# Masked attention's inputs loaded during the quantised stage's second loop, and its preparation and loop made one block

## The chip, the cores and the metric

The kernel runs on one core of a Trainium2 chip. The metric is the device time of one execution in microseconds (us), lower being better; the runs give a median.

## What is computed

Four layers are applied in turn to x (2 sequences of 2048 rows of 512), each with a layer norm ahead and a residual add behind:

```python
x = x + _L0_xattn_ref(_layernorm(x), ctx_1024, ctx_1024, mask_BxS2_bf0, ...)    # rope attention, causal
x = x + _L0_ffn_ref(_layernorm(x), clip_x, clip_down, w_gate, w_up, w_down)     # quantised gated FFN
x = x + _L1_xattn_ref(_layernorm(x), ctx_1024, ctx_1024, mask_1x1xSxS2_bk0, ...) # masked attention
x = x + _L1_ffn_ref(_layernorm(x), Wg, bg, We, be)                              # 8 experts, one per row
```

The change is about the third, whose keys and values come from ctx (2 x 128 rows of 512):

```python
Q = _split_heads(q @ Wq.T + bq); K = _split_heads(k @ Wk.T + bk); V = _split_heads(v @ Wv.T + bv)
scores = jnp.einsum('bhqd,bhkd->bhqk', Q, K) / math.sqrt(DV)      # 16 heads of 32
scores = jnp.where(mask, 1e-09, scores); attn = jax.nn.softmax(scores, axis=-1)
ctx = jnp.einsum('bhqk,bhkd->bhqd', attn, V)
return ctx.transpose(0, 2, 1, 3).reshape(b, -1, 512) @ Wo.T + bo
```

The second layer quantises its hidden values with one scale taken over all of them, so it needs two loops over the rows: the first makes the hidden values and their peak, the second rounds them and multiplies by the down weights.

## The kernel before

There is one program of four stages. Each stage is one or two blocks; a block holds one straight list of instructions for each engine (TensorE is PE, VectorE DVE, ScalarE ACT, GpSimd POOL, SyncE SP, which issues the loads and stores), and all engines meet at a barrier between two blocks. Within a block engines wait for one another through counted semaphores alone, so the order in which the lists are written is the order of the work. The rows `xres` (4096 rows in 32 tiles of 128) stay in SBUF throughout.

**The quantised stage's second loop** (in `quantised_ffn_stage`, block at L1302) goes over 8 chunks q of 512 rows. The hidden values of a chunk take 2816 KB; three chunks are kept in SBUF (`hidden`, three buffers), and five come back from HBM (L1310). The reload for chunk q is issued when ACT and DVE have rounded chunk q - 3 (`whole_by_act`, `whole_by_dve`), so it goes into the buffer that this chunk leaves. For each chunk ACT rounds it in two pieces (L1326), DVE clamps (L1367), ACT and DVE write it out as whole numbers in bf16 (L1340, L1360, L1362), PE multiplies (44 matmuls, L1423), DVE scales the result (L1375) and POOL or DVE adds it to `xres`. After the fifth reload SP has nothing more to do in the block.

**The masked stage** (`masked_attention_stage`) is two blocks. In the first (L1552), the preparation, SP issues all loads: ctx, wk, three small ones, wv, wq, wo, and three that the expert stage needs later (`router`). PE turns ctx (8 transposes, L1609), ACT copies the result out as `ctxT` (L1570), PE makes the keys (32 matmuls, L1616) and the values (16, L1622); ACT and DVE split `wq` and `wo` into a high and a low part for the three-product matmuls (L1578, L1587, L1580, L1595). In the second block (L1639), the loop, the first rows are prepared: DVE and POOL norm four tiles (L1770 to L1782, POOL the power at L1659), PE turns two (`turn_x`, L1886), ACT casts them to the high part (L1697) and DVE makes the low part (L1788), PE makes the first chunk's queries (`project`, 48 matmuls, L1879 to L1881), turns two more tiles, and the loop over 16 chunks of 256 rows begins.

PE's results go through four PSUM banks used in turn. `PRE` lists who empties the use of a bank in the preparation, in the order in which PE fills them; PE waits ahead of use u for the emptying of use u - 4 (`begin`, `pre_begin`). SBUF under the preparation's inputs is later taken by the loop's tiles (`probs` and others).

## Time and profile before

| | |
|---|---|
| median of 3 runs | 1639.64 us (1638.8 to 1640.21) |
| the profiled execution | 1640.35 us |
| its span, first to last instruction | 1638.2 us |
| PE, DVE, ACT, POOL busy | 93%, 72%, 54%, 30% of the span |
| quantised stage, second loop | 856 to 941 us |
| masked stage: preparation | 941 to 966 us |
| masked stage: first rows | 966 to 986 us |
| masked stage: loop | 986 to 1370 us |

Times in the rows below count from the span's start. A row of the timeline gives the start, the length, the engine, the line, what is written and read, and in brackets how long the engine had been idle and what released it. PEld is PE's weight load, which runs beside the matmuls. The clock column is PE's granted clock as a share of 2.4 GHz; it has two levels, 2.4 and 1.2 GHz (1.00 and 0.50).

### The profile page before, as it was taken

Reading aid. Unit: us, or ns where it says so; the run is one execution under the profiler, and the core shown is the slowest. Engines: PE = TensorE matmul, PEld = TensorE weight load, DVE = VectorE, ACT = ScalarE, POOL = GpSimd, SP = SyncE. Lnnn points to the kernel's source line nnn. Section 1 sums busy time; section 2 is a strip of 40 time slices with the busy share of each in tenths; the row PEclk is TensorE's granted clock in tenths of the full one; section 3 lists DMA queues with packets and bytes.
Section 4 is the critical chain, followed back from the end, with each engine's and each line's share of the span. In section 5 each row is a group of like instructions: output and inputs, shape, how many; then the busy total and the mean of one; then the engine's idle time right before and its main releaser. Section 6 shows DMA issues by size and latency. Waiting matters only on the chain. (4 is left out here: it accounts for less than half of the span.)

```text
span 1638.2 us, 31002 instructions
## 1 busy us (share of the span) xinstructions
PE 1522.3 (93%) x11022; PEld 1126.2 (69%) x11022; DVE 1182.3 (72%) x2306; ACT 886.4 (54%) x2091; POOL 492.5 (30%) x436
## 2 busy tenths in 40 slices
PE   6699999999999999699989968999999997998997
PEld 4567777777777776444444447888888875886785
DVE  4458778786777565488878736877878765778876
ACT  1344433444344434466659427888888884665342
POOL 0122222232222222100004513445454533665333
PEclk9899999999999999799999978999999998999999
DMA  6501111110110101133107140000000005215741
GB/s 244 190 14 42 50 61 49 42 38 7 34 39 33 42 7 72 42 133 142 80 1 290 64 165 3 4 2 3 3 3 3 1 2 201 116 72 170 213 149 66
DMA packets 47275, 118.29 MB, mean 72 GB/s; under 512 B 9406, under 2 KB 15934, under 8 KB 45504
## 3 DMA queue, kind: packets, MB, share of 16 engines
q1 hardware_dynamic: 41488, 100.03, 17.3%
q0 software_dynamic: 5680, 16.85, 2.6%
q8 instruction: 65, 1.06, 0.3%
q14 instruction: 42, 0.34, 0.1%
HBM read 78.89 MB, written 39.80 MB: 72 GB/s over the span
## 5 line engine op out<-in xcount | busy, mean ns | idle before, releaser
L1711 ACT ACTIVATE c_probs<-c_score,c_minus_top 128x128 f32<-128x128 f32 x512 | 182.7, 387 | 0.9 <-DVE c_minus_top L1799 0.8
L605 POOL TENSOR_TENSOR a_attn_lo_parts<-a_attn,a_attn_hi_parts 128x512 fp32r<-128x512 f32 x64 | 80.2, 1286 | 250.0 <-ACT a_attn_hi_parts L671 250.0
L1671 POOL TENSOR_TENSOR c_probs<-c_probs,c_recip 128x1024 f32<-128x1024 f32 x64 | 121.5, 1899 | 45.2 <-DVE c_recip L1805 45.2
L667 ACT COPY a_attn<-a_pv_ps 128x512 f32<-128x512 f32 x64 | 36.9, 577 | 162.6 <-PE a_pv_ps L941 162.6
L1711 ACT ACTIVATION_READ_ACCUMULATOR c_probs<-c_score,c_minus_top 128x1 f32 x512 | 115.8, 226 | 0.0
L904 PE MATMUL a_bank<-a_x_hi_parts,a_wq_hi 128*128 128x256 f32 x512 | 107.8, 293 | 4.7 <-POOL a_x_lo_parts L601 4.7
L904 PE MATMUL a_bank<-a_x_lo_parts,a_wq_hi 128*128 128x256 f32 x512 | 104.3, 286 | 0.0
L904 PE MATMUL a_bank<-a_x_hi_parts,a_wq_lo 128*128 128x256 f32 x512 | 104.0, 285 | 0.0
L631 ACT ACTIVATE a_q<-a_bank,a_shift,a_gain 128x256 f32<-128x256 f32 x64 | 32.3, 556 | 130.2 <-PE a_bank L895 130.2
L887 PE MATMUL a_bank<-a_wo_hi,a_attn_hi_parts 128*128 128x512 f32 x256 | 102.3, 400 | 0.0
L2190 ACT CAST d_xT_hi<-d_turn 128x512 fp32r<-128x512 f32 x71 | 41.7, 587 | 110.2 <-PE d_turn L2434 102.5
L888 PE MATMUL a_bank<-a_wo_lo,a_attn_hi_parts 128*128 128x512 f32 x256 | 101.1, 395 | 0.0
L889 PE MATMUL a_bank<-a_wo_hi,a_attn_lo_parts 128*128 128x512 f32 x256 | 100.5, 393 | 0.0
L1796 DVE COPY_PREDICATED_SCALAR c_score<-c_masks,c_tiny 128x1024 f32 x64 | 82.1, 1283 | 25.1 <-issue 25.1
L1257 PE MATMUL b_gate<-b_xT,ahead_gateT 128*128 128x512 bf16 x352 | 91.9, 384 | 3.5 <-ACT b_xT L1135 3.5
L601 POOL TENSOR_TENSOR a_x_lo_parts<-a_q,a_x_hi_parts 128x512 fp32r<-128x512 f32 x32 | 43.0, 1364 | 167.0 <-ACT a_x_hi_parts L637 167.0
L1159 ACT ACTIVATE b_silu<-b_gate,ahead_scale 128x512 f32<-128x512 f32 x88 | 60.2, 685 | 59.7 <-PE b_gate L1257 59.7
L904 PEld LDWEIGHTS a_bank<-a_x_hi_parts,a_wq_hi 128*128 128x128 f32 x512 | 80.3, 193 | 17.6 <-issue 11.8
L1215 DVE SCALAR_TENSOR_TENSOR b_hidden<-b_up,ahead_scale,b_silu 128x512 f32<-128x512 f32 x88 | 65.8, 747 | 35.6 <-PE b_up L1257 35.5
L1705 ACT COPY c_probsT<-c_bank 128x512 f32<-128x512 f32 x128 | 69.1, 593 | 41.0 <-PE c_bank L1937 33.4
L1257 PE MATMUL b_up<-b_xT,ahead_upT 128*128 128x512 bf16 x352 | 91.2, 382 | 0.0
L651 ACT ACTIVATE a_probs<-a_score_ps 128x1024 f32<-128x1024 f32 x64 | 65.8, 1027 | 40.1 <-PE a_score_ps L926 40.1
(302 smaller groups left out, 4365.0 us busy)
## 6 DMA issues: line engine op xcount, KB each, us to landing
hidden<-b_hidden SPq DMA_DIRECT2D x5, 2816.0 KB, 8.1
b_hidden<-hidden SPq DMA_DIRECT2D x5, 2816.0 KB, 10.1
xres<-in_x SPq DMA_DIRECT2D x8, 1024.0 KB, 14.1
d_we<-in_we SPq DMA_DIRECT2D x8, 1024.0 KB, 12.8
xres<-in_w_gate_up SPq DMA_DIRECT2D x7, 1024.0 KB, 5.2
d_got<-rows SPq DMA_DIRECT2D x20, 258.0 KB, 3.1
xres<-rows SPq DMA_DIRECT2D x19, 258.0 KB, 2.8
a_rot<-in_rot SPq DMA_DIRECT2D x16, 256.0 KB, 3.1
```

The lines of the kernel that those rows point to most:

```text
L605: nc.gpsimd.tensor_tensor(of_spread(attn_lo, g), of_spread(attn, g), of_spread(attn_hi, g), ALU.subtract).then_inc(attn_lo_ready, 1)
L651: nc.scalar.activation(buf, score_ps[:, p % 2], ACT.Tanh, scale=1.0 / (DH0 ** 0.5 * GROK)).then_inc(capped, 1)
L887: nc.tensor.matmul(out, hi, w_hi, start=first, stop=False)
L888: nc.tensor.matmul(out, hi, w_lo, start=False, stop=False)
L889: return nc.tensor.matmul(out, lo, w_hi, start=False, stop=last)
L904: last = nc.tensor.matmul(out[:, i, :], w[:, k, cols], x[:, k, :], start=(j == 0 and i == 0), stop=(j == len(products) - 1 and i == 1))
L1215: nc.vector.scalar_tensor_tensor(hidden[:, n % KEPT, i, :], up_ps[:, u % RING, :], up_scale[:, i:i + 1], silu[:, u % RING, :], ALU.mult, A ...
L1257: last = nc.tensor.matmul(ps[:, u % RING, :], w[:, k, i * P:(i + 1) * P], xT[:, n % 2, k, :], start=(k == 0), stop=(k == KB - 1))
L1671: nc.gpsimd.tensor_tensor(part, part, recip[:, t % 2, heads].unsqueeze(2).to_broadcast([P, HALF, KEYS]), ALU.mult).then_inc(scaled, 1)
L1705: nc.scalar.copy(probsT[:, QUADS * h:QUADS * h + QUADS, :].rearrange("p h t -> p (h t)"), out[:]).then_inc(freed["act"], 1)
L1711: last = nc.scalar.activation(probs[:, t, at, :], score_ps[:, h, g, :], ACT.Exp, bias=minus_top[:, h, g:g + 1], accum_out=total[:, t, at:a ...
L1796: ch.step(nc.vector.copy_predicated(part, masks[:, j, t, :].unsqueeze(1).to_broadcast(shape), tiny[:].unsqueeze(2).to_broadcast(shape)))
```

## The change

1. `MaskedAhead` gives ctx, wk, wv, the small inputs, wq, wo and `ctxT` fixed places in SBUF: wq and wo in `front`, which the second loop doesn't use, the rest over `hidden` buffers that the last chunks leave.
2. SP issues those loads in the quantised stage's second loop: wq and wo right after the first reload and ahead of the second; ctx, wk and wv after chunk 5 has been rounded, the small ones after chunk 6.
3. The preparation's block and its barrier are gone: its instructions stand at the head of the loop's block. The loads for the expert stage are issued there first, and the masks' after them.
4. The first two tiles are turned between the keys and the values, `PRE` follows, and DVE norms those tiles ahead of everything else.

```diff
--- before.py
+++ after.py
+MASKED_OFFSET = 172800
+class MaskedAhead:
...
+        size = 4 * KB * D
+        self.offset = offset
+        self.wk, self.wv = at("wk", [P, KB, D], offset), at("wv", [P, KB, D], offset + size)
+        self.turned_offset = offset + 2 * size
+        self.ctx, self.ctxT = at("ctx", [P, B, D], self.turned_offset), at("ctxT", [P, KB, B * KEYS], self.turned_offset + 4 * B * D)
+        small = offset + 3 * size
+        self.bv, self.bo, self.bias = at("bv", [P, D], small), at("bo", [P, D], small + 4 * D), at("bias", [P, 2, KB], small + 8 * D)
+        self.end = small + 8 * D + 32
+        self.wq, self.wo = at("wq", [P, KB, D], front_offset), at("wo", [P, KB, D], front_offset + 4 * TPC * ROW)
+        self.ld_ctx, self.ld_small, self.ld_wk, self.ld_wv, self.ld_wq, self.ld_wo = (
+            whole.enter_context(nc.semaphore("masked_ld_" + x)) for x in ("ctx", "small", "wk", "wv", "wq", "wo"))
...
@@ -1308,6 +1333,23 @@
...
                         sp.dma_start(hidden[:, b].rearrange("p i t -> p (i t)"), io["hidden"][n]).then_inc(reloaded[b], 16)
+                        if q == KEPT:
+                            for tile, name, loaded in ((masked.wq, "wq1", masked.ld_wq), (masked.wo, "wo1", masked.ld_wo)):
+                                sp.dma_start(tile[:], io[name].rearrange("(k p) n -> p k n", p=P)).then_inc(loaded, 16)
+
...
+                    sp.wait_ge(whole_by_act, CHUNKS - 3)
+                    sp.wait_ge(whole_by_dve, whole_here(CHUNKS - 3))
+                    sp.dma_start(masked.ctx[:], io["ctx"].rearrange("(b p) f -> p b f", p=P)).then_inc(masked.ld_ctx, 16)
+                    for tile, name, loaded in ((masked.wk, "wk1", masked.ld_wk), (masked.wv, "wv1", masked.ld_wv)):
+                        sp.dma_start(tile[:], io[name].rearrange("(k p) n -> p k n", p=P)).then_inc(loaded, 16)
+                    sp.wait_ge(whole_by_act, CHUNKS - 2)
+                    sp.wait_ge(whole_by_dve, whole_here(CHUNKS - 2))
+                    sp.dma_start(masked.bias[:], io["qk_bias"]).then_inc(masked.ld_small, 16)
+                    sp.dma_start(masked.bv[:], io["bv"].partition_broadcast(P)).then_inc(masked.ld_small, 16)
+                    sp.dma_start(masked.bo[:], io["bo"].partition_broadcast(P)).then_inc(masked.ld_small, 16)
...
-        bias = sb("bias", [P, 2, KB])
-        bo = sb("bo", [P, D])
+        bias, bv, bo = masked.bias, masked.bv, masked.bo
+        wk, wv, wq, wo, ctx_t, ctxT = masked.wk, masked.wv, masked.wq, masked.wo, masked.ctx, masked.ctxT
+        ld_ctx, ld_small, ld_wk, ld_wv, ld_wq, ld_wo = masked.ld_ctx, masked.ld_small, masked.ld_wk, masked.ld_wv, masked.ld_wq, masked.ld_wo
...
-        PRE = ["act"] * KB + ["act"] * KB + ["dve"] * B + ["dve"] * NT + ["act"] * KB + ["dve"] * NT
-        PRE_K, PRE_V, PRE_T = KB, 2 * KB, 2 * KB + B
-        PRE_Q, PRE_T2 = PRE_T + NT, PRE_T + NT + KB
+        PRE = ["act"] * KB + ["act"] * KB + ["dve"] * NT + ["dve"] * B + ["act"] * KB + ["dve"] * NT
+        PRE_K, PRE_T, PRE_V = KB, 2 * KB, 2 * KB + NT
+        PRE_Q, PRE_T2 = PRE_V + B, PRE_V + B + KB
...
-        with ExitStack() as early:
...
-            with nc.Block() as block:
-                @block.sync
-                def _(sp):
-                    sp.dma_start(ctx_t[:], io["ctx"].rearrange("(b p) f -> p b f", p=P)).then_inc(ld_ctx, 16)
-                    for tile, name, s in ((wk, "wk1", ld_wk), (wv, "wv1", ld_wv), (wq, "wq1", ld_wq), (wo, "wo1", ld_wo)):
-                        sp.dma_start(tile[:], io[name].rearrange("(k p) n -> p k n", p=P)).then_inc(s, 16)
...
-                    sp.dma_start(router.wg[:], io["wg"].rearrange("(k p) n -> p k n", p=P)).then_inc(router.loaded, 16)
...
-                @block.scalar
...
-                        if g == 1:
-                            act.wait_ge(ld_wq, 16)
-                            nc.scalar.copy(wq_hi[:], wq[:]).then_inc(weight_hi, 1)
-                    act.wait_ge(ld_wo, 16)
-                    nc.scalar.copy(wo_hi[:], wo[:]).then_inc(weight_hi, 1)
-
...
-                @block.vector
...
-                    dve.wait_ge(weight_hi, 2)
-                    nc.vector.tensor_tensor(wo_lo[:], wo[:], wo_hi[:], ALU.subtract).then_inc(weight_lo, 1)
...
-                @block.tensor
-                def _(pe):
...
-                    pe.wait_ge(ld_ctx, 16)
...
+        assert next_offset(nc) <= masked.offset
+        sb("loaded", [P, (masked.end - next_offset(nc)) // 4])
+        assert next_offset(nc) == masked.end
+        probs = nc.alloc_sbuf_tensor_at("c_probs", [P, 2, H1, KEYS], F32, offset=masked.offset)
+        probsT = nc.alloc_sbuf_tensor_at("c_probsT", [P, H1, P], F32, offset=masked.turned_offset)
...
-        probs = sb("probs", [P, 2, H1, KEYS])
-        probsT = sb("probsT", [P, H1, P])
...
+                sp.dma_start(router.wg[:], io["wg"].rearrange("(k p) n -> p k n", p=P)).then_inc(router.loaded, 16)
+                sp.dma_start(router.bg_or_row[:, 0:D], io["bg"].partition_broadcast(P)).then_inc(router.loaded, 16)
+                sp.dma_start(router.tables[:], io["tables"]).then_inc(router.loaded, 16)
                 all_chunks(sp, body)
...
+                for k in range(KB):
+                    act.wait_ge(bank_full, k + 1)
+                    nc.scalar.copy(ctxT[:, k, :], bank[k % NB][:, 0:B * KEYS]).then_inc(freed["act"], 1)
+                act.wait_ge(ld_wq, 16)
+                nc.scalar.copy(wq_hi[:], wq[:]).then_inc(weight_hi, 1)
+                act.wait_ge(ld_small, 48)
+                for g in range(QUADS):
+                    act.wait_ge(bank_full, PRE_K + g + 1)
+                    nc.scalar.activation(keys[:, :, g, :], bank[(PRE_K + g) % NB][:, 0:B * KEYS].rearrange("p (b k) -> p b k", b=B),
+                                         ACT.Identity, bias=bias[:, 1, g:g + 1]).then_inc(freed["act"], 1)
                 for t in range(NT):
                     x_high(t, 0, t, PRE_T + t + 1, bank[(PRE_T + t) % NB])
+                act.wait_ge(ld_wo, 16)
+                nc.scalar.copy(wo_hi[:], wo[:]).then_inc(weight_hi, 1)
...
+                nc.vector.memset(tiny[:], 1e-9).then_inc(set_up, 1)
+                dve.wait_ge(set_up, 1)
                 for tile in range(NT):
                     norm_stats(tile, tile % 2, True)
                     norm_row(tile, tile % 2, True)
+                dve.wait_ge(weight_hi, 1)
+                nc.vector.tensor_tensor(wq_lo[:], wq[:], wq_hi[:], ALU.subtract).then_inc(weight_lo, 1)
+                dve.wait_ge(ld_small, 48)
+                nc.vector.tensor_scalar(q_bias[:], bias[:, 0, :], scale_by, None, ALU.mult).then_inc(bias_ready, 1)
+                for tile in range(NT):
+                    x_low(tile, 0, tile, bank[(PRE_T + tile) % NB])
                 for tile in range(NT, 2 * NT):
                     norm_stats(tile, tile % 2)
                     norm_row(tile, tile % 2)
-                for tile in range(NT):
-                    x_low(tile, 0, tile, bank[(PRE_T + tile) % NB])
+                for b in range(B):
+                    dve.wait_ge(bank_full, PRE_V + b + 1)
+                    nc.vector.tensor_tensor(vals[:, b], bank[(PRE_V + b) % NB][:].rearrange("p (h d) -> p h d", d=DH1),
+                                            bv[:].rearrange("p (h d) -> p h d", d=DH1), ALU.add).then_inc(freed["dve"], 1)
+                dve.wait_ge(weight_hi, 2)
+                nc.vector.tensor_tensor(wo_lo[:], wo[:], wo_hi[:], ALU.subtract).then_inc(weight_lo, 1)
                 for tile in range(NT):
                     x_low(NT + tile, 1, tile, bank[(PRE_T2 + tile) % NB])
...
-                pe.wait_ge(weight_lo, 1)
+                pe.wait_ge(ld_ctx, 16)
+                for k in range(KB):
+                    out = pre_begin(k)
+                    for b in range(B):
+                        last = nc.tensor.transpose(out[:, b * KEYS:(b + 1) * KEYS], ctx_t[:, b, k * P:(k + 1) * P], ident[:])
+                    last.then_inc(bank_full, 1)
+                pe.wait_ge(freed["act"], KB)
+                pe.wait_ge(ld_wk, 16)
+                for m in range(KB):
+                    out = pre_begin(PRE_K + m)
+                    for k in range(KB):
+                        last = nc.tensor.matmul(out[:, 0:B * KEYS], wk[:, k, m * P:(m + 1) * P], ctxT[:, k, :], start=(k == 0), stop=(k == KB - 1))
+                    last.then_inc(bank_full, 1)
                 for t in range(NT):
                     turn_x(t, t, pre_begin(PRE_T + t))
-                pe.wait_ge(freed["dve"], ring.count("dve", PRE_Q))
+                pe.wait_ge(ld_wv, 16)
+                for b in range(B):
+                    out = pre_begin(PRE_V + b)
+                    for k in range(KB):
+                        last = nc.tensor.matmul(out[:], ctxT[:, k, b * KEYS:(b + 1) * KEYS], wv[:, k, :], start=(k == 0), stop=(k == KB - 1))
+                    last.then_inc(bank_full, 1)
+                pe.wait_ge(weight_lo, 1)
+                pe.wait_ge(freed["dve"], ring.count("dve", PRE_V))
                 for m in range(KB):
                     project(pre_begin(PRE_Q + m), 0, m)
```

The instructions' order shows the moves at three places. The first is PE's list from the end of the quantised stage to the first query matmul (`c_bank` are the four PSUM banks, `xn` the normed rows). Before:

```order
L1609 MATMUL c_bank<-ident,c_ctx 128x128 [waits c_ld_ctx]
...
L1616 MATMUL c_bank<-c_ctxT,c_wk 128x256 [waits c_freed_by_act,c_ld_wk]
...
L1622 MATMUL c_bank<-c_wv,c_ctxT 128x512 [waits c_freed_by_act,c_ld_wv]
...
L1622 MATMUL c_bank<-c_wv,c_ctxT 128x512 [waits c_freed_by_act]
...
L1552 UNCONDITIONAL_BRANCH
L1865 UNCONDITIONAL_BRANCH [waits barrier_Pool_Activation_PE_DVE_SP_release]
L1886 MATMUL c_bank<-ident,c_xn 128x128 [waits c_xn_ready,c_freed_by_act,c_weight_lo]
...
L1886 MATMUL c_bank<-ident,c_xn 128x128 [waits c_xn_ready,c_freed_by_act]
...
L1879 MATMUL c_bank<-c_x_hi_parts,c_wq_hi 128x256 [waits c_freed_by_dve]
```

and with the change (lines are those of the changed file):

```order
L1904 MATMUL c_bank<-ident,masked_ctx 128x128 [waits masked_ld_ctx]
...
L1911 MATMUL c_bank<-masked_ctxT,masked_wk 128x256 [waits c_freed_by_act,masked_ld_wk]
...
L1880 MATMUL c_bank<-ident,c_xn 128x128 [waits c_xn_ready,c_freed_by_act]
...
L1880 MATMUL c_bank<-ident,c_xn 128x128 [waits c_xn_ready,c_freed_by_act]
...
L1919 MATMUL c_bank<-masked_wv,masked_ctxT 128x512 [waits c_freed_by_act,masked_ld_wv]
...
L1919 MATMUL c_bank<-masked_wv,masked_ctxT 128x512 [waits c_freed_by_act]
...
L1873 MATMUL c_bank<-c_x_hi_parts,c_wq_hi 128x256 [waits c_freed_by_dve,c_weight_lo]
```

The two groups that read `c_xn` have moved from behind the barrier to the place between the keys (L1911) and the values (L1919), and the query matmuls now stand right behind the values; the branch and the barrier between are gone, and the wait for `weight_lo` has moved from the turns to the first query matmul.

The second place is DVE's list over the same stretch, without the memsets and the small steps within a norm. Before:

```order
L1587 TENSOR_TENSOR c_wq_lo<-c_wq,c_wq_hi 128x2048 [waits c_weight_hi,c_set_up]
L1589 TENSOR_SCALAR c_q_bias<-c_bias 128x4 [waits c_ld_small]
L1592 TENSOR_TENSOR c_vals<-c_bank,c_bv 128x512 [waits c_bank_full] x2
L1595 TENSOR_TENSOR c_wo_lo<-c_wo,c_wo_hi 128x2048 [waits c_weight_hi]
L1552 UNCONDITIONAL_BRANCH
L1762 UNCONDITIONAL_BRANCH [waits barrier_Pool_Activation_PE_DVE_SP_release]
L1770 BN_STATS c_stats<-xres 128x6
...
L1782 TENSOR_SCALAR c_xn<-xres,c_mv,c_rstd 128x512 [waits c_rstd_ready]
L1770 BN_STATS c_stats<-xres 128x6
```

and with the change:

```order
L1751 BN_STATS c_stats<-xres 128x6 [waits c_set_up]
...
L1763 TENSOR_SCALAR c_xn<-xres,c_mv,c_rstd 128x512 [waits c_rstd_ready]
...
L1810 TENSOR_TENSOR c_wq_lo<-masked_wq,c_wq_hi 128x2048 [waits c_weight_hi]
L1812 TENSOR_SCALAR c_q_bias<-masked_bias 128x4 [waits masked_ld_small]
L1769 TENSOR_TENSOR c_x_lo_parts<-c_bank,c_x_hi_parts 128x4x128 [waits c_x_hi] x2
L1751 BN_STATS c_stats<-xres 128x6 [waits c_xn_ready]
...
L1763 TENSOR_SCALAR c_xn<-xres,c_mv,c_rstd 128x512 [waits c_x_hi,c_rstd_ready]
...
L1820 TENSOR_TENSOR c_vals<-c_bank,masked_bv 128x512 [waits c_bank_full] x2
L1823 TENSOR_TENSOR c_wo_lo<-masked_wo,c_wo_hi 128x2048 [waits c_weight_hi]
```

The first two tiles' norms have moved ahead of the split of wq, and the low parts of those tiles ahead of the norms of the next two; the values' additions and the split of wo come last.

The third place is SP's list (the DMA issues) from the second loop on. Before, the masked stage's began behind the barrier:

```order
L1555 DMA c_ctx<-in_ctx 128x2x512
L1557 DMA c_wk<-in_wk 128x4x512
L1559 DMA c_bias<-in_qk_bias 128x8
...
L1557 DMA c_wv<-in_wv 128x4x512
L1557 DMA c_wq<-in_wq 128x4x512
L1557 DMA c_wo<-in_wo 128x4x512
L1562 DMA router_wg<-in_wg 128x4x512
L1563 DMA router_bg<-in_bg 128x512
L1564 DMA router_tables<-in_tables 128x271
```

and with the change, from the first reload (L1335) on:

```order
L1335 DMA b_hidden<-hidden 128x5632 [waits b_whole_by_dve,b_whole_by_act,b_spilled0]
L1338 DMA masked_wq<-in_wq 128x4x512
L1338 DMA masked_wo<-in_wo 128x4x512
L1335 DMA b_hidden<-hidden 128x5632 [waits b_whole_by_dve,b_whole_by_act,b_spilled1]
...
L1345 DMA masked_ctx<-in_ctx 128x2x512 [waits b_whole_by_dve,b_whole_by_act]
L1347 DMA masked_wk<-in_wk 128x4x512
L1347 DMA masked_wv<-in_wv 128x4x512
L1350 DMA masked_bias<-in_qk_bias 128x8 [waits b_whole_by_dve,b_whole_by_act]
...
L1615 DMA router_wg<-in_wg 128x4x512
...
L1613 DMA c_masks<-in_mask 128x2x128
```

The two 128x4x512 loads of wq and wo now stand between the first and the second reload in the same queue, the others behind the last reload, and the first masks behind the router's loads.

## Rows read from the trace of the kernel before

**Rows 1.** The page of the profile: the span.
```profile
span 1638.2 us, 31002 instructions
```

**Rows 2.** Busy time by stretch: us, PE, PEld, DVE, ACT, POOL (instructions), clock, DMA share, GB/s.
```profile
941.00:986.00 45.00, 27.98 (x117) 21.37 (x118) 14.14 (x28) 9.89 (x16) 7.48 (x9) 0.77 0.42 150
986.00:1364.00 378.00, 367.39 (x3769) 318.85 (x3767) 286.39 (x518) 304.77 (x1275) 171.93 (x120) 0.98 0.01 3
```

**Rows 3.** Timeline of PE: start us, length, line, names; last, idle before and releaser.
```profile
944.76 1.97 PE L1609 MATMUL c_bank<-ident,c_ctx 128*128 128x128 f32 x8 [5.41 <-DMA c_ctx<-in_ctx]
947.60 8.89 PE L1616 MATMUL c_bank<-c_ctxT,c_wk 128*128 128x256 f32 x32 [0.88 <-ACT c_ctxT L1570]
956.33 7.03 PE L1622 MATMUL c_bank<-c_wv,c_ctxT 128*128 128x512 f32 x16
969.21 1.08 PE L1886 MATMUL c_bank<-ident,c_xn 128*128 128x128 f32 x4 [5.85 <-DVE c_xn L1782]
...
977.91 0.58 PE L1879 MATMUL c_bank<-c_x_hi_parts,c_wq_hi 128*128 128x256 f32 x1 [5.39 <-DVE c_x_lo_parts L1788]
...
985.48 1.03 PE L1886 MATMUL c_bank<-ident,c_xn 128*128 128x128 f32 x8
...
994.92 1.57 PE L1903 MATMUL c_score<-c_keys,c_q 32*128 32x128 f32 x16 [1.43 <-ACT c_probs L1711]
```

**Rows 4.** Timeline of DVE at the boundary and after the second barrier.
```profile
939.39 0.69 DVE L1375 TENSOR_TENSOR b_delta<-b_out,b_down_row 128x512 f32<-128x512 f32 x1 [1.68 <-PE b_out L1423]
...
941.16 0.06 DVE L1584 MEMSET c_tiny<- 128x1 f32 x1 [0.35 <-PEq L1302]
956.84 2.29 DVE L1587 TENSOR_TENSOR c_wq_lo<-c_wq,c_wq_hi 128x2048 fp32r<-128x2048 f32 x1 [15.63 <-ACT c_wq_hi L1578]
...
966.60 0.69 DVE L1770 BATCH_NORM_STATS2 c_stats<-xres 128x6 f32<-128x512 f32 x1 [0.32 <-PEq L1552]
...
968.52 0.55 DVE L1782 TENSOR_SCALAR c_xn<-xres,c_mv,c_rstd 128x512 f32<-128x512 f32 x1 [0.81 <-POOL c_rstd L1659]
...
976.58 1.27 DVE L1788 TENSOR_TENSOR c_x_lo_parts<-c_bank,c_x_hi_parts 128x512 fp32r<-128x512 f32 x2
```

**Rows 5.** Timeline of POOL and ACT in the preparation.
```profile
975.11 5.16 POOL L1665 TENSOR_TENSOR xres<-xres,c_bo 128x512 f32<-128x512 f32 x4
...
945.48 1.65 ACT L1570 COPY c_ctxT<-c_bank 128x256 f32<-128x256 f32 x4 [20.53 <-PE c_bank L1609]
```

**Rows 6.** Timeline at the barrier ahead of the quantised stage.
```profile
670.90 0.32 SPq L1104 DMA_DIRECT2D b_down_scales<-down_scale  x1
...
670.96 2.06 PE L213 MATMUL b_gate<-ahead_ident,ahead_rows 128*128 128x128 bf16 x20 [2.94 <-PEq L542]
```

**Rows 7.** Busy time and granted clock in short stretches.
```profile
944.00:945.00 1.00, 0.24 (x1) 0.24 (x2) 0.00 (x0) 0.00 (x0) 0.00 (x0) 0.66 1.06 412
951.00:952.00 1.00, 1.00 (x5) 0.82 (x5) 0.00 (x0) 0.47 (x1) 0.00 (x0) 0.93 1.04 404
981.00:982.00 1.00, 1.00 (x7) 1.00 (x6) 0.00 (x0) 0.41 (x1) 0.00 (x0) 0.57 0.00 0
994.00:996.00 2.00, 1.08 (x14) 1.08 (x16) 1.91 (x3) 2.00 (x12) 0.69 (x2) 0.88 0.00 0
1002.00:1004.00 2.00, 2.00 (x23) 1.88 (x24) 0.76 (x2) 1.76 (x9) 2.00 (x2) 0.92 0.00 0
```

**Rows 8.** One line (L1310), the reloads: the DMA time to landing, and one issue.
```profile
DMA to landing us min/median/max: 9.4/10.1/10.5
...
871.15 0.32 SPq L1310 DMA_DIRECT2D b_hidden<-hidden  x1
```

**Rows 9.** Timeline of ACT and DVE in the quantised stage's second loop.
```profile
887.33 5.36 ACT L1326 ACTIVATE b_hidden<-b_hidden,b_magic_h,b_h_inv 128x2560 f32<-128x2560 f32 x2
894.35 2.43 ACT L1340 ACTIVATE b_whole_h<-b_hidden,b_minus_magic 128x2560 bf16<-128x2560 f32 x1 [1.67 <-DVE b_hidden L1367]
...
901.40 0.69 DVE L1375 TENSOR_TENSOR b_delta<-b_out,b_down_row 128x512 f32<-128x512 f32 x1 [1.07 <-PE b_out L1423]
```

More of the change, by code:

```diff
@@ L1039, in _, with quantised_ffn_stage @@
                 chunks(pe, body)
-def quantised_ffn_stage(nc, io, xres, front_offset, seen, ahead):
+def quantised_ffn_stage(nc, io, xres, front_offset, seen, ahead, masked):
     with ExitStack() as stage:
@@ L1435, with masked_attention_stage @@
 MASK_CPB = MASK_CHUNKS // B
-def masked_attention_stage(nc, io, xres, ident, seen, router):
+def masked_attention_stage(nc, io, xres, ident, seen, masked, router):
     NT, NC, NB = MASK_TILES, MASK_CHUNKS, 4
@@ L2517, in build_program @@
         router = RouterAhead(nc, whole)
+        masked = MaskedAhead(nc, whole, front_offset, MASKED_OFFSET)
         rope_attention_stage(nc, io, xres, front_offset, ident, seen, ahead)
-        quantised_ffn_stage(nc, io, xres, front_offset, seen, ahead)
-        masked_attention_stage(nc, io, xres, ident, seen, router)
+        quantised_ffn_stage(nc, io, xres, front_offset, seen, ahead, masked)
+        masked_attention_stage(nc, io, xres, ident, seen, masked, router)
         expert_stage(nc, io, xres, front_offset, ident, seen, router)
```

68 lines of the change are left out of this document (11 added, 57 removed).

## The prediction

> **What bounds the kernel now.** I took the page first, for the span [rows 1], and then busy time by stretch. From 986 to 1364 us PE is busy 367.39 of 378 us at clock 0.98; from 941 to 986 us it is busy 27.98 of 45 us at clock 0.77 [rows 2]. The masked stage's loop is therefore bound by PE, and what can be had lies in the 45 us ahead of it, which is where the change works. The loop's first steps need the first chunk's queries, so the number to follow is the end of the query matmuls: 985.48 us, where PE goes over to the next turns [rows 3]. Whatever that moves by, the loop, the expert stage and the end move by, unless something is given back later.
>
> PE's timeline shows how those 45 us go [rows 3]. It ends the quantised stage about 939.4 us (DVE takes its last result at 939.39), and the block behind the barrier begins with DVE's memset at 941.16 [rows 4]. PE starts at 944.76, released by the load of ctx. It turns ctx, makes keys (947.60) and values (956.33 to 963.36). Then it is idle, but for two turns of a tile, until 977.91: DVE splits the weights, the barrier falls (DVE's first norm is at 966.60 [rows 4]), DVE and POOL norm four tiles one after the other, and only then come the two low parts (976.58) for which the queries wait. The queries take 7.57 us, half of that at the low clock.
>
> **The change, part by part.**
>
> *The loads are gone from the head of the stage.* PE's first turn waits for nothing but the barrier. At the barrier ahead of the quantised stage PE had work ready and began at 670.96, with SP at 670.90 [rows 6]; so I let it start at 941.1. Removed: 944.76 - 941.1 = 3.7 us. ACT's split of wq (it had waited for its load) now runs while PE makes the keys.
>
> *The first rows are turned between keys and values, and the second barrier is gone.* The norms begin at 941.2 instead of 966.60. One tile took from 966.60 to 968.52 + 0.55 = 969.07, 2.5 us, so two are ready by 946.2, ahead of the end of the keys. The split of wq follows on DVE (2.29 us [rows 4]), done by 948.5, also hidden by the keys. From the values' start to the queries' start was 977.91 - 956.33 = 21.6 us. It becomes two tiles' turns (eight transposes at full clock took 1.03 us [rows 3]) and the values' 7.03: 8.0 us. Removed: 13.6 us. For this the low parts (1.27 us for both [rows 4]) and the casts ahead of them must fit under the values' 7.0 us, which leaves 5.7 us for two casts. What was between them and the turns, the norms of tiles 2 and 3 (2 x 2.5 us), now comes behind them on DVE and is due only after the queries.
>
> *The queries at the full clock.* They ran from 977.91 to 985.48, the clock at 0.57 for 981 to 982 [rows 7], so it rose at 981.9. Those 4.0 us at half clock become about 2.0. PE will have come from 7 us of unbroken values. Removed: 1.9 us.
>
> *The order of ACT and DVE.* I look for what is late next. DVE, in turn: low parts done by about 955.5, norms of two tiles (5.0 us, 960.5), the two additions of the values, which the third and fourth group of queries need for their banks, and the split of wo (about the 2.29 us of wq's), done by 964.5. The queries run from 960.5 to 966.2, so their third group, at 963.4, finds its bank emptied at about 961.2, and the fourth's too. Nobody waits for the split of wo before the third tile's output. POOL's 5.16 us of adding `bo` [rows 5] follow the fourth power and end about 965.5; POOL then waits for the loop. All of this costs nothing, but its cover is thin, 2 us: if DVE were 3 us later, the queries would wait for 1 us.
>
> *SP's queue.* Wq and wo go between the first and the second reload. The second was issued at 871.15 and a reload lands after at most 10.5 us [rows 8], 881.65. The two loads are 2048 KB, a reload is 2816 KB in 10.1 us; at that rate they put it off by 7.3 us, to 889.0; if they fit into gaps of the queue, by nothing. ACT takes that chunk up at 887.33, so 1.6 us may show. But it ends it at 894.35 + 2.43 = 896.78, and PE comes to that chunk at about 901.3 (DVE takes the last result of the one before at 901.40) [rows 9]: 4.5 us of slack. Cost: nothing. The other loads go into an empty queue at about 908 and 918 us, and nothing reads them before 941. The first masks come behind the router's three loads, issued at 941 and first used behind the queries, 25 us later. Nothing.
>
> A rule speaks against that part. The Trainium skill, "DMA: Bandwidth & Descriptors", section "Queues, rings and completion order", says that descriptors of one queue are consumed in ring order on each DMA engine. By it the second reload gets the whole delay, 7.3 us, rather than nothing; by the slack just named the sum is the same.
>
> *The clock in the keys.* It fell at 944.3 (0.66 of 944 to 945), 5 us after PE stopped, and rose at 951.1 (0.93 of 951 to 952) [rows 7]; the keys' first 3.5 us and the turn of ctx were at 1.2 GHz. PE's pause is now 1.7 us instead of 5.4. If the clock stays up, the keys give 1.8 us and the turns some 0.3 (ACT's 1.65 us of copies [rows 5] set the rest): up to 2.1. If it falls, nothing, since from the turn of ctx to the values all goes as before. The nearest row is a pause of 1.43 us that ended at 994.92 [rows 3]: the clock fell at 995.5 (0.88 of 994 to 996) [rows 7]. That is nearer to what comes, so I take little: 0.3 us.
>
> *Sum.* 3.7 + 13.6 + 1.9 + 0.3 = 19.5 us. The span becomes 1638.2 - 19.5 = 1618.7, and the profiled execution 1640.35 - 19.5 = 1620.85. That execution is 0.7 above the median, 1639.64, so I say 1620.1 for the median. Without the last term it is 1620.4, with all of it 1618.3.
>
> **The rivals.**
>
> *Another dip of the clock more or less* (chance 0.22). After this preparation PE ran at half clock from 995.5 to 1002.3 (0.92 of 1002 to 1004) [rows 7] in the loop's first chunk, which costs 6.8 / 2 = 3.4 us. The loop starts at another moment now. Without that dip 1617; with a second one 1623.5.
>
> *PE starts no earlier* (0.07). Each engine enters a new list of instructions at the barrier; the 3.7 us of waiting for ctx covered whatever it needs for that. If it needs all of it, that term is zero and the time is 1623.8. Against it stands the start at 670.96. This would be a stall for instruction fetch, of which the Trainium skill ("Runtime: NRT & Kernel Launch", section "Instruction fetch mechanics") says that a taken branch out of the pages at hand stops the engine until the target is fetched. By that rule 1623.8, by the row of the earlier barrier 1620.1.
>
> *DVE or ACT is late for the queries* (0.05). The whole split of wo (2.3 us) or one norm (2.5 us) lands on the path: 1622.5.
>
> *The second reload comes too late, and the kernel is slower* (0.02). What must happen: the loads of wq and wo hold the second reload back by more than the margins before it, 887.33 - 881.65 = 5.7 and 4.5 us, 10.2 us in all, and then by the 19.5 us gained. So it decides from a delay of 29.7 us on, four times the 7.3 that their bytes are worth. With 12 us of delay it costs 2 us: 1622. Against it: each later reload is issued only when a chunk is rounded, so delays don't pile up.
>
> *The change does not do what it says* (0.02): some input is waited for all the same, and PE idles as before; no change, 1639.6. Nothing in the rows speaks for it but that a load can be late; the last is issued 20 us ahead.
>
> **How the numbers follow.** The forecast has 0.62. Its own range is 1618.3 to 1621.5; the dips widen it to 1617 and 1623.5, and an entry stall to 1623.8. Both together, an entry stall and a dip, or a piece of DVE's work beside one, reach 1625.5, and a dip saved beside a clock that stays up 1615.5. I give 1615.5 to 1625.5. All cases but the last two are faster by over 0.2% (3.3 us, about what a measurement of this kernel can tell from no change): 0.96; same 0.02; slower 0.02.
>
> **What the changed profile would show.** PE's first turn of ctx at 941.1 and not released by a DMA; keys to 952 or 953; turns of `xn` with no idle ahead of them; values to about 960.5; the first query matmul right behind at clock 1.00, with no wait for DVE; the turns after the queries at 966. In the second loop PE's matmuls without a gap, as before, and ACT's rounding of chunk 4 at 887 to 889. The prediction is wrong if PE waits for the low parts or for a bank, if the second loop ends after 941.5, or if the loop from the first chunk to the end takes more than 3.5 us longer or shorter than the 652.7 us from 985.48 to the end.

## The result, and the profile after

The changed kernel takes 1615.07 us (median of 4 runs, 1613.59 to 1616.49) against 1639.61 in the same comparison: ratio 0.985, 95% interval 0.983 to 0.987. Two more comparisons on other occasions gave 0.985 again (below). The gain is 24.5 us; 19.5 were forecast, and the range ended at 1615.5.

The page of the kernel after, its span:

```profile
span 1611.9 us, 30968 instructions
```

Busy time of the kernel after in the two stretches that answer to [rows 2], now 22 us for what took 45, and the loop:

```profile
939.00:961.00 22.00, 21.37 (x111) 16.43 (x112) 13.95 (x28) 9.15 (x15) 9.20 (x9) 1.00 0.22 69
961.00:1344.00 383.00, 368.83 (x3787) 319.19 (x3785) 288.68 (x522) 306.28 (x1276) 172.25 (x122) 0.99 0.01 3
```

Timeline of PE after, which answers to [rows 3]:

```profile
863.27 73.91 PE L1465 MATMUL b_out<-b_downT,b_whole_h 128*128 128x512 bf16 x335 [0.22 <-issue]
938.96 1.06 PE L1904 MATMUL c_bank<-ident,masked_ctx 128*128 128x128 f32 x8 [1.77 <-PEq L1327]
940.65 7.17 PE L1911 MATMUL c_bank<-masked_ctxT,masked_wk 128*128 128x256 f32 x32 [0.63 <-ACT masked_ctxT L1691]
947.67 1.04 PE L1880 MATMUL c_bank<-ident,c_xn 128*128 128x128 f32 x8
948.54 7.03 PE L1919 MATMUL c_bank<-masked_wv,masked_ctxT 128*128 128x512 f32 x16
955.01 0.68 PE L1873 MATMUL c_bank<-c_x_hi_parts,c_wq_hi 128*128 128x256 f32 x1
...
961.16 1.04 PE L1880 MATMUL c_bank<-ident,c_xn 128*128 128x128 f32 x8
...
970.60 1.16 PE L1897 MATMUL c_score<-c_keys,c_q 32*128 32x128 f32 x16 [1.44 <-ACT c_probs L1680]
972.99 1.97 PE L1934 MATMUL c_bank<-ident,c_probs 128*128 128x128 f32 x8 [1.23 <-POOL c_probs L1640]
```

No row from the keys to the turns behind the queries has a bracket: PE waits 1.77 us behind the barrier and 0.63 us for `ctxT`, then for nothing. The second loop's matmuls have no gap in their last 74 us. The turn of ctx is released by PE's own sequencer (PEq), no longer by a DMA.

SP and ACT after, in the second loop, which answer to [rows 8] and [rows 9]:

```profile
862.06 0.32 SPq L1335 DMA_DIRECT2D b_hidden<-hidden  x1
862.43 0.43 SPq L1338 DMA_DIRECT2D masked_wq<-in_wq  x1
862.90 2.12 SPq L1338 DMA_DIRECT2D masked_wo<-in_wo  x1
869.04 28.39 SPq L1335 DMA_DIRECT2D b_hidden<-hidden  x4
```

```profile
885.22 5.34 ACT L1368 ACTIVATE b_hidden<-b_hidden,b_magic_h,b_h_inv 128x2560 f32<-128x2560 f32 x2
```

The second reload, issued at 869.04, took 15.2 us instead of about 10 and landed at 884.2, 1.0 us ahead of ACT, whose row has no bracket: 5 of the 5.7 us of the first margin went, and nothing shows.

The expert stage begins here after (at 1370.17 us before):

```profile
1344.01 1.90 ACT L2221 CAST d_wg_hi<-router_wg 128x2048 fp32r<-128x2048 f32 x1 [5.58 <-PEq L1605]
```

The profiled executions, stage by stage (us; from the rows above and those of [rows 3]):

| | before | after | gained |
|---|---|---|---|
| PE begins the second loop (code unchanged ahead of it) | 859.62 | 857.52 | 2.1 |
| PE's pause ahead of the turn of ctx | 5.41 | 1.77 | 3.64 |
| turn of ctx to keys | 2.84 | 1.69 | 1.15 |
| keys to what follows | 8.73 | 7.02 | 1.71 |
| values' start (two turns ahead, in after) to queries | 21.58 | 7.34 | 14.24 |
| queries to the turns behind them | 7.57 | 6.15 | 1.42 |
| those turns to the expert stage's first row | 384.7 | 382.85 | 1.8 |
| that row to the end | 268.0 | 267.9 | 0.1 |

The five rows of the boundary make 22.2 us, and with the loop and the end 24.1; the medians give 24.5, and four runs of the changed kernel lie over 2.9 us. The 2.1 us ahead of the change are in these two executions only (below).

### The profile page after: what moved, and what is told of

Its sections match the earlier page's. It is cut to its first block and busy times, and to the rows that moved or that the text cites. A ratio compares the mean times of both kernels' runs of the same rounds, so it can differ in the third digit from the quotient of the medians.

```text
span 1611.9 us, 30968 instructions
## 1 busy us (share of the span) xinstructions
PE 1510.6 (94%) x10998; PEld 1118.0 (69%) x11022; DVE 1182.0 (73%) x2306; ACT 886.7 (55%) x2091; POOL 494.5 (31%) x436
```

## The experiments

All are against the kernel before in the same comparison (its median 1639.6 to 1640.7). Table of what each trace shows; the column "half" is the time at half clock in the loop's first 28 us, its first chunk and a little of the second, and "tail" goes from the turns behind the queries to the end of the span.

| kernel | median, ratio [95%] | PE's pause at the barrier | first turn to turns behind the queries | half | tail |
|---|---|---|---|---|---|
| before | 1639.64 | 5.41 | 40.7 | 10.2 | 652.7 |
| before again | 1639.46, 0.9999 [0.999, 1.001] | 5.28 | 40.7 | 10.2 | 652.55 |
| after | 1615.07, 0.985 [0.983, 0.987] | 1.77 | 22.2 | 3.4 | 650.7 |
| after again | 1615.49, 0.985 [0.983, 0.986] | 1.77 | 22.2 | 3.4 | 650.8 |
| after, third | 1615.02, 0.985 [0.984, 0.987] | 1.78 | 22.2 | 3.4 | 650.8 |
| loads only | 1632.46, 0.996 [0.995, 0.997] | 1.77 | 37.7 | 10.2 | 652.4 |
| turned behind | 1619.78, 0.987 [0.986, 0.989] | 1.78 | 24.0 | 3.4 | 652.3 |
| ctx late | 1622.27, 0.989 [0.987, 0.991] | 5.88 | 24.7 | 3.4 | 651.1 |
| filler x4 | 1625.39, 0.991 [0.989, 0.993] | 1.77 | 22.2 | 3.4 | 650.7 |
| filler x8 | 1638.01, 0.9986 [0.9977, 0.9996] | 1.77 | 22.2 | 3.4 | 650.75 |
| pause 3 | 1619.58, 0.988 [0.987, 0.990] | 3.05 | 23.9 | 3.4 | 649.8 |
| pause 4 | 1618.76, 0.987 [0.986, 0.989] | 4.41 | 23.4 | 3.4 | 650.7 |
| pause ahead of the queries | 1627.1, 0.992 [0.990, 0.994] | 1.77 | 29.5 | 10.2 | 654.2 |

**Before again, after again, after a third time.** Both kernels unchanged.

> The kernel before, unchanged, run and profiled again. Theory A (the time above the forecast came from the boundary alone: TensorE's clock stayed at 2.4 GHz there) expects this profile to agree with the first one to 0.5 us at the end of the quantised stage's second loop (941 us) and in the masked loop's first chunk. Theory B (part of the gain beyond the forecast is the moments at which the clock falls early in the program and early in the masked loop, which differ from execution to execution) expects those marks to move by 1 to 3 us without any change of the program, with the sum of half-clock time other than 103 us.

> The changed kernel, unchanged, run and profiled again. Four runs gave 1613.6 and 1616.4 us, two each. Theory A expects one level in the mean of many runs near 1615 us and the boundary as in the first profile (PE from 938.96 to 961.16 us, 22.2 us, no fall of the clock). Theory B expects again two groups about 2.8 us apart, and a profile whose second loop ends about 939 or about 941 us.

> The changed kernel once more, on the same chip as the three others, as their base. 1615.5 as in the run before, within 1.5 us. From the barrier ahead of the masked block to the turns behind the queries 22.2 us again, at full clock without a dip; the moment at which the second loop ends may lie anywhere from 938.9 to 942 us, since it moved between executions of one kernel. If the clock falls at that barrier in this execution, then the 2.9 us hang on chance and not on the length of the pause.

PE began the second loop at 858.62 in the second trace of before, and at 859.24 and 858.35 in the two of after, where the first pair had 859.62 and 857.52. Over all the traces of this study the same code began there between 857.5 and 862.6. So the 2.1 us ahead of the change are the scatter of single executions and no gain; why they scatter wasn't tried. The boundary took 22.2 us and the loop's first chunk had its 3.4 us at half clock in all three traces of after.

**Loads only.** The loads are issued in the second loop as in the change, but the preparation and the loop stay two blocks in the order of before.

```diff
+                        if q == KEPT:
+                            for tile, name, loaded in ((masked.wq, ...), (masked.wo, ...)):
+                                sp.dma_start(tile[:], ...).then_inc(loaded, 16)
...
+                    sp.dma_start(masked.ctx[:], ...).then_inc(masked.ld_ctx, 16)
...
-                    sp.dma_start(ctx_t[:], ...).then_inc(ld_ctx, 16)
```

> Only the loads are moved into the second loop; the preparation keeps its own block and its order. If TensorE's clock stays up after the shorter pause (theory A), the gain is the 3.7 us of waiting for ctx and 2.9 us of clock in the turns and keys: 6.6 us, 1633.0 us. By the forecast's own terms, with 0.3 us for the clock, it is 4.0 us, 1635.6 us. If the change is worth something only as a whole (the barrier behind the preparation eats what the loads give), it is under 1 us, 1639 us.

Timeline of its PE:

```profile
941.22 1.07 PE L1640 MATMUL c_bank<-ident,masked_ctx 128*128 128x128 f32 x8 [1.77 <-PEq L1327]
942.92 7.17 PE L1647 MATMUL c_bank<-masked_ctxT,masked_wk 128*128 128x256 f32 x32 [0.63 <-ACT masked_ctxT L1601]
949.93 7.03 PE L1653 MATMUL c_bank<-masked_wv,masked_ctxT 128*128 128x512 f32 x16
962.81 1.09 PE L1921 MATMUL c_bank<-ident,c_xn 128*128 128x128 f32 x4 [5.85 <-DVE c_xn L1817]
...
971.50 0.58 PE L1914 MATMUL c_bank<-c_x_hi_parts,c_wq_hi 128*128 128x256 f32 x1 [5.38 <-DVE c_x_lo_parts L1823]
```

It gains 7.5 us by the medians and 6.7 by the ratio, near the 6.6 of a wait and a clock that is saved, and away from the 4.0 of the forecast's terms. The keys take 7.17 us here too, with the order of before around them, so it is the loads and not the one block that keep the clock up.

**Turned behind.** The one block, but the two tiles are turned behind the values instead of ahead of them, and DVE adds up the values ahead of the low parts.

```diff
-                for t in range(NT):
-                    turn_x(t, t, pre_begin(PRE_T + t))
                 pe.wait_ge(ld_wv, 16)
...
+                for t in range(NT):
+                    turn_x(t, t, pre_begin(PRE_T + t))
```

> The changed kernel in one block, with the first two tiles turned behind the values, as the order was before (DVE adds the values first). Theory A: PE waits behind the turns for one cast (0.6 us) and one low part (0.7 us), so 1.3 to 2 us slower than the changed kernel, about 1616.8 us. The rival, that turning ahead is what brings most of the 13.6 us between the values and the queries, expects 5 us or more, 1620 us or above.

```profile
957.92 1.04 PE L1880 MATMUL c_bank<-ident,c_xn 128*128 128x128 f32 x8
960.52 0.39 PE L1873 MATMUL c_bank<-c_x_hi_parts,c_wq_hi 128*128 128x256 f32 x1 [1.56 <-DVE c_x_lo_parts L1769]
966.38 1.04 PE L1880 MATMUL c_bank<-ident,c_xn 128*128 128x128 f32 x8
...
970.40 0.39 PE L1873 MATMUL c_bank<-c_x_hi_parts,c_wq_hi 128*128 128x256 f32 x1 [1.90 <-DVE c_x_lo_parts L1769]
```

PE waits 1.56 us for the low parts, which in the changed kernel hide under the values, and the boundary takes 1.8 us more, as theory A had it. Another 1.5 us are lost in the first chunk, where DVE is behind (1.90 us ahead of the next queries against 0.47 in the changed kernel). The two make 3.4 us; the medians differ by 4.3 to 4.8. The median, 1619.78, is 3.0 us over theory A's time and just under the 1620 of its rival, so A was right on the wait ahead of the queries and had nothing for the first chunk. Turning ahead is worth 3.4 us or a little more, 1.8 of it at the boundary. The rest of the 14.2 is the second barrier and the norms behind it: without them, but with the tiles turned behind the values, the boundary is 24.0 us, in loads only 37.7.

**Ctx late.** The changed kernel, with ctx alone loaded at the head of the masked block.

```diff
-                    sp.dma_start(masked.ctx[:], ...).then_inc(masked.ld_ctx, 16)
                     for tile, name, loaded in ((masked.wk, ...), (masked.wv, ...)):
...
+                sp.dma_start(masked.ctx[:], ...).then_inc(masked.ld_ctx, 16)
                 sp.dma_start(router.wg[:], ...).then_inc(router.loaded, 16)
```

> The changed kernel with one load put back: ctx is asked for at the head of the masked block, as before the change; everything else (the one block, the order, the other five loads) stays. Theory A (the short pause at the barrier leaves the clock up, the long one lets it fall): PE waits 5.3 us or more for ctx, the granted clock falls to half ahead of the turn of ctx and rises about 7 us later; from the end of the wait to the keys' start 2.8 us instead of 1.7, the keys take 8.7 us instead of 7.2. So 3.7 us of wait and 2.9 us of clock are given back: 6.6 us over the changed kernel, about 1622. Theory B (the 2.9 us came from the order of ACT's and DVE's work beside the keys, not from the length of the pause): the turn and the keys stay at 1.7 and 7.2 us and only the wait comes back: 3.7 us, about 1619. In both, the values, the turns and the queries behind the keys stay as in the changed kernel, since the clock is up again by then: 14.3 us from the values' start to the turns behind the queries.

Timeline of its PE, and its clock in two stretches:

```profile
944.15 1.97 PE L1904 MATMUL c_bank<-ident,masked_ctx 128*128 128x128 f32 x8 [5.88 <-DMA masked_ctx<-in_ctx]
946.58 8.89 PE L1911 MATMUL c_bank<-masked_ctxT,masked_wk 128*128 128x256 f32 x32 [0.46 <-ACT masked_ctxT L1691]
955.31 1.04 PE L1880 MATMUL c_bank<-ident,c_xn 128*128 128x128 f32 x8
```

```profile
942.00:951.00 9.00, 6.38 (x21) 5.16 (x22) 4.39 (x8) 3.76 (x6) 0.61 (x2) 0.62 0.59 219
951.00:969.00 18.00, 18.00 (x95) 13.61 (x94) 8.57 (x15) 5.68 (x9) 8.39 (x6) 1.00 0.00 1
```

1622.27, 7.2 us over the changed kernel in the same comparison; 6.6 was theory A's, 3.7 theory B's. In the trace the wait is 4.1 us longer and the stretch from the first turn 2.5 us: the keys are slow again, with the one block and its order around them.

**Filler x4 and x8.** Four or eight more transfers of 1 MB stand between the first reload and wq's; nobody reads them, and the last small loads wait for them.

```diff
                         if q == KEPT:
+                            for i in range(4):
+                                sp.dma_start(io["filler"][i], io["we"][i]...).then_inc(filled, 16)
```

> The changed kernel with four more transfers of 1 MB each (a copy from one place of the chip's memory to another, read by nobody) between the first reload and the loads of wq and wo, so the second reload stands behind 6 MB instead of 2 MB. In the changed kernel the second reload lands 22.2 us after the first was issued, 7680 KB in all, 346 KB a us, 1.0 us before ACT takes its chunk up, and PE has about 4.5 us more. Theory A (the queue is served in order and is full there): 4096 KB more are 11.8 us more, less 5.5 of margin is 6 us of idle PE in the second loop; about 1621. With a copy at the rate of the lone reload (279 KB a us) 14.7 less 5.5, 9 us; about 1624. Theory B (the loads go into gaps and delay nothing): no gap on PE, 1615.

> The same with eight transfers of 1 MB, so 10 MB ahead of the second reload. Theory A: 8192 KB at 346 KB a us are 23.7 us, less 5.5 of margin is 18 us of idle PE in the second loop, about 1633; at 279 KB a us 24 us, about 1639, and once PE is idle that long the clock falls with it and a few us come on top. Theory B: 1615. The step from four to eight, 12 to 15 us by theory A, gives the price of a MB in this queue without the margin in it.

ACT and PE of filler x4, then of filler x8:

```profile
899.40 5.36 ACT L1372 ACTIVATE b_hidden<-b_hidden,b_magic_h,b_h_inv 128x2560 f32<-128x2560 f32 x2 [13.95 <-DMA b_hidden<-hidden]
...
907.22 37.95 PE L1469 MATMUL b_out<-b_downT,b_whole_h 128*128 128x512 bf16 x166 [8.02 <-ACT b_whole_h L1386]
```

```profile
912.39 5.36 ACT L1372 ACTIVATE b_hidden<-b_hidden,b_magic_h,b_h_inv 128x2560 f32<-128x2560 f32 x2 [25.13 <-DMA b_hidden<-hidden]
...
920.22 24.97 PE L1469 MATMUL b_out<-b_downT,b_whole_h 128*128 128x512 bf16 x107 [18.97 <-ACT b_whole_h L1386]
```

Theory B is out. The second reload landed 37.2 and 48.4 us after the first was issued (899.40 - 862.19, 912.39 - 864.02), against 22.2 in the changed kernel: the first 4 MB delay it by 15.0 us, the next 4 by 11.2. Most of the delay comes before the reload is in the queue at all, as SP's rows of filler x4 and then of filler x8 show:

```profile
862.56 10.10 SPq L1339 DMA_DIRECT2D filler<-in_we  x4
...
878.69 30.32 SPq L1336 DMA_DIRECT2D b_hidden<-hidden  x4
```

```profile
864.38 20.48 SPq L1339 DMA_DIRECT2D filler<-in_we  x8
...
893.93 28.08 SPq L1336 DMA_DIRECT2D b_hidden<-hidden  x4
```

SP needs 10.1 and 20.5 us to issue the fillers, and so issues the second reload 16.5 and 29.9 us after the first instead of 7.0 (869.04 - 862.06). That is 9.5 of the 15.0 us and 22.9 of the 26.2; the rest lies between its issue and its landing. PE idled 8.0 and 19.0 us, so 7.0 and 7.2 us of delay were hidden; with the 5 us that wq and wo had used, the margin is 12 us where the forecast had 10.2. The kernels are 10.4 and 23.0 us slower than the changed one in the same comparison: the idle time and, in either trace, 2.1 us more up to the turn of ctx, where the clock was low behind it; of filler x8's, 1.9 us are not accounted for. The medians, 1625.39 and 1638.01, are nearest to theory A's times at the rate of a lone reload, 1624 and 1639. A page of the Trainium skill, "DMA: Bandwidth & Descriptors", section "Queues, rings and completion order", has the descriptors of a queue served in ring order on each DMA engine; the traces fit that, with 15.2 us from issue to landing for the second reload behind 2 MB, instead of about 10, and 20.7 and 18.5 in the fillers' traces. They don't show the order of the descriptors themselves.

**Pause 3 and pause 4.** The changed kernel with one wait more ahead of PE's first turn of ctx: for DVE's first variance (`var_ready`), or for its first normalised tile (`xn_ready`).

```diff
+                pe.wait_ge(var_ready, 1)
                 pe.wait_ge(ld_ctx, 16)
```

> The changed kernel with one wait more: PE's first turn of ctx waits for DVE's first variance, which in the changed kernel was there 1.2 us after PE began. So PE's pause at the barrier is 3.0 us instead of 1.8; nothing else changes. Theory A1 (what counts is how long PE pauses, and the clock falls only close to the 5.4 us seen before): the clock stays up, the keys take 7.2 us, and the kernel is 1.2 us slower than the changed one, about 1616.3. Theory A2 (it falls from a pause of some 3 us on): the keys take 8.7 us and the turn is slower, 2.9 us more, about 1619.

> The same with the wait for DVE's first normalised tile, which ended 2.6 us after PE began: PE's pause is 4.4 us. With the clock up: 2.6 us slower than the changed kernel, about 1617.8. If the clock falls: 2.9 us more, about 1620.7. Together with 1.8 us (up) and 5.4 to 5.9 us (down) the two say between which pauses at this barrier the clock is lost, and so what the forecast's last term hung on.

PE and the clock of pause 3, then PE of pause 4:

```profile
941.54 1.10 PE L1905 MATMUL c_bank<-ident,masked_ctx 128*128 128x128 f32 x8 [3.05 <-DVE c_var L1756]
943.27 8.86 PE L1912 MATMUL c_bank<-masked_ctxT,masked_wk 128*128 128x256 f32 x32 [0.63 <-ACT masked_ctxT L1691]
```

```profile
942.00:947.00 5.00, 4.37 (x15) 3.40 (x14) 3.96 (x7) 2.99 (x5) 0.81 (x2) 0.66 0.78 280
947.00:965.00 18.00, 18.00 (x93) 13.54 (x92) 8.99 (x17) 6.15 (x10) 7.73 (x6) 1.00 0.01 1
```

```profile
941.65 1.52 PE L1905 MATMUL c_bank<-ident,masked_ctx 128*128 128x128 f32 x8 [4.41 <-DVE c_xn L1763]
943.64 8.12 PE L1912 MATMUL c_bank<-masked_ctxT,masked_wk 128*128 128x256 f32 x32 [0.46 <-ACT masked_ctxT L1691]
```

The clock fell in both, for 3.4 us (0.66 of 5 us in pause 3), and not for the 6.8 us that pauses of 5.3 to 5.9 had. It cost 1.7 and 1.2 us in the boundary, so theory A2 has the fall right and its price too high. In the traces the two are 3.0 and 3.9 us longer than the changed kernel up to the turns behind the queries; the medians, 1619.58 (4 runs over 6 us) and 1618.76, don't tell the two apart, and of pause 4 the median lies between the forecasts with the clock up and fallen, so it is the trace that decides. At this barrier the clock is kept with a pause of 1.77 or 1.78 us (in eight traces of six kernels), and lost with 3.05 and 4.41, in one trace each. In the five traces in which it fell there it did so 4.7 to 5.0 us after PE had stopped, in pause 3 and pause 4 when PE was already at work again; that is some evidence against mere chance of the moment, though not a proof.

**A pause ahead of the queries.** The changed kernel, with the queries waiting for both splits of the weights.

```diff
-                pe.wait_ge(weight_lo, 1)
+                pe.wait_ge(weight_lo, 2)
```

> The changed kernel with PE's queries made to wait for DVE's split of wo, which in the changed kernel ended 4.0 us after the queries began; nothing else changes. So PE pauses some 3.5 us ahead of the queries, as it paused 5.4 and more there before the change, and enters the loop's first chunk with that history. In both theories the clock falls in the queries (it fell from a pause of 3.0 us at the barrier): 4.0 us of wait and about 1.7 us of clock, 28 us from PE's first turn to the turns behind the queries instead of 22.2. Theory A (the loop's 1.9 us came from the idle PE ahead of it: a low clock there is followed by one low stretch more in the first chunk): 6.8 or more us at half clock in the first chunk instead of 3.4, and from the turns behind the queries to the end some 652.5 us instead of 650.8; about 1622.5. Theory B (they came from the order of the one block): one stretch of 3.4 us as in the changed kernel, 650.8 us or less, since DVE is then ahead of PE; about 1620.5.

Timeline of its PE, and its clock at the queries and in the first chunk:

```profile
965.06 0.58 PE L1873 MATMUL c_bank<-c_x_hi_parts,c_wq_hi 128*128 128x256 f32 x1 [4.54 <-DVE c_wo_lo L1823]
973.42 1.03 PE L1880 MATMUL c_bank<-ident,c_xn 128*128 128x128 f32 x8
```

```profile
963.00:971.00 8.00, 5.94 (x28) 5.95 (x29) 2.00 (x1) 0.89 (x2) 3.13 (x1) 0.57 0.00 0
973.00:983.00 10.00, 7.72 (x75) 6.70 (x76) 7.52 (x13) 6.74 (x23) 1.82 (x2) 1.00 0.03 5
983.00:995.00 12.00, 10.75 (x68) 10.11 (x69) 7.52 (x15) 6.42 (x29) 5.57 (x4) 0.57 0.00 0
```

Theory A: the first chunk has 10.2 us at half clock instead of 3.4 (0.57 of 12 us). Before and loads only have the same 10.2 there, but in two stretches of 6.8 and 3.4 us, here it is one. The tail is 3.4 us longer, 2.7 of it in the loop and the rest in the expert stage, where this trace has one more stretch of 3.4 us at half clock. The median is 12 us over the changed kernel, where theory A had 7.5: 1.5 more at the boundary (29.5 us instead of 28) and 1.7 more in the tail; 1.3 are not accounted for. This is one trace.

## Why the prediction was too high

*The loads are gone from the head of the stage:* right. PE's first turn waits 1.77 us behind the barrier (1.7 forecast) and for no DMA; 3.64 us against 3.7. Ctx late gave the wait back. There is no entry stall beyond those 1.8 us.

*The first rows turned between keys and values, and the queries at the full clock:* right, 14.24 + 1.42 = 15.7 us against 13.6 + 1.9 = 15.5. The low parts fitted under the values, and the first query follows them with no bracket. The two terms are off by 0.6 and 0.5 us in opposite senses because rows of PE overlap: the values' row, 948.54 + 7.03 = 955.57, ends 0.56 us past the start of the queries' first at 955.01, so that start came early and the queries are that much longer.

*The order of ACT and DVE:* right. DVE ended the values' additions and the split of wo by 959; no query waits for a bank.

```profile
955.51 1.27 DVE L1820 TENSOR_TENSOR c_vals<-c_bank,masked_bv 128x512 f32<-128x512 f32 x2
956.71 2.27 DVE L1823 TENSOR_TENSOR c_wo_lo<-masked_wo,c_wo_hi 128x2048 fp32r<-128x2048 f32 x1
```

*SP's queue:* right. The second reload was 5 us late (between nothing and the 7.3 forecast), the margins covered it, and the fillers priced both: 15.0 us for the first 4 MB, 12 us of margin. The rival of a slower kernel was said to decide at 29.7 us of delay; filler x8, 31 us in all (26.2 and the 5 of wq and wo), came out at 0.9986 of before. What kept it on the near side is the 5 us more of gain and the 2 us more of margin, less the clock behind the pause.

*The clock in the keys:* this step failed. "That is nearer to what comes, so I take little: 0.3 us" sized it by a pause of 1.43 us in the loop, at whose end the clock fell [rows 3, 7]. At the barrier it didn't fall, and the turns and keys gave 1.15 + 1.71 = 2.9 us. The row was the nearest in length only. It is not shown which of its surroundings makes the difference, but they differ: around it PE waits several times over (the changed kernel has 1.44 and 1.23 us within 3 us there, at 970.60 and 972.99, and the clock falls there as well); ahead of the barrier PE had been busy without a gap for 74 us. The most that it was allowed, 2.1, had the keys right (1.8 against 1.71) and the turn too small (0.3 against 1.15 from its start to the keys'). What the runs put in its place: a single pause of 1.77 us behind busy work costs no clock, one of 3.05 or 4.41 costs 1.2 to 1.7 us, one of 5.3 to 5.9 costs 2.5 to 2.9. The trace of before had a row nearer in kind: at the barrier ahead of the quantised stage, which the forecast used for PE's start [rows 6], PE paused once, for 2.94 us, behind some 11 us of work without a gap, and the clock fell 0.3 us after it had started again:

```profile
670.00:672.00 2.00, 1.04 (x13) 1.07 (x14) 1.58 (x10) 0.22 (x1) 0.54 (x2) 0.81 0.05 6
```

It fell there in all 13 traces, with pauses of 2.94 or 2.95 us, in two of them just ahead of PE's start. So a single pause behind busy work costs the clock at 2.9 us and doesn't at 1.8; no run tried one in between. The forecast's pause of 1.7 us was shorter than that row and longer than the loop's 1.43, and the trace of before alone didn't decide between nothing and 2.1: 0.3 was a choice and no reading.

*Another dip of the clock more or less:* it was a rival with chance 0.22, either way alike, and came true in part: 6.8 us less at half clock in the first chunk, worth 1.8 us where 3.4 was said. The forecast saw 6.8 us there (995.5 to 1002.3); before has another 3.4 behind it, from 1009.5, and it is this pair that becomes one stretch of 3.4. Some 27 us into the loop the changed kernel is 2.4 us ahead (1014.28 - 985.48 against 987.54 - 961.16, both at the same `c_score` matmuls) and 1.8 at its end; part of a slower clock goes into waits that PE has anyway, but that split was not measured. It was not chance: the first chunk had 10.2 us at half clock in the four traces in which PE had paused for 4.5 us or more ahead of the queries or the turns just before them, and 3.4 in the nine others, and the pause ahead of the queries, in its one trace, turned one into the other. By the mechanism, less idle PE ahead of the loop, this rival should have been part of the forecast, on its better side alone.

So 19.5 becomes 3.6 + 15.7 + 2.9 + 1.8 = 24.0. With the clock's term right the forecast would have been 1617.5, inside its range, and with the loop's as well 1615.6, at its edge. That the median fell just outside, at 1615.07, is the 0.5 us between the rows and the medians, which is less than single runs scatter (1613.59 to 1616.49); on which side of 1615.5 it came to lie was luck.

Open: why the second loop begins between 857.5 and 862.6 in executions of the same code, and what decides when the clock falls, beyond these pauses: whether it is the waits close by or the busy stretch ahead that parts the barrier's 1.77 us, where it stays up, from the loop's 1.43, where it falls, was not tried.

## What to carry to other kernels

When an edit shortens a wait of PE, price the clock as well as the wait: the low stretch behind it may count as gained if the pause that is left is short, single and behind busy work (1.77 us here, not 2.94), and low stretches further on, in work that the edit doesn't touch, may go with it. Choose the row that such a price is taken from by what stands around it, not by its length alone. A load put ahead of an urgent one in the same queue delays it (2 MB by 5 us here, 4 MB more by 15), partly because the issuing engine itself is held up, so first add up the slack of everything between that transfer and the engine that sets the time.

## What was not expected of the hardware

At the same barrier a pause of PE of 1.77 us left the granted clock at 1.00 and one of 3.05 us brought it to half for 3.4 us, in one trace, one of 5.88 for 6.8. In the loop's first chunk it falls behind pauses of 1.44 and 1.23 us. A pause of 4.54 us ahead of the queries was followed by 6.8 us at half clock in the queries and, after 13.5 us at full clock, by 10.2 us in a chunk that has 3.4 without it.

Copies of 1 MB within the chip's memory delayed a reload of the same queue by 15.0 us for the first four and 11.2 for the next four, 273 and 366 KB a us, beside 279 for a reload alone; SP took 10.1 us to issue the first four and 20.5 to issue all eight.
